# Second attention of a fused four-layer block: scores in pairs of heads

## The reference, cut to what matters

```python
# query: 8 x 112 x 512 (normalized x), key_value: 8 x 375 x 512 (context), 16 heads of 32
Q = query @ Wq.T + bq
K = key_value @ Wk.T + bk
V = key_value @ Wv.T + bv
# Q, K, V -> (batch, head, token, 32)
scores = jnp.einsum('bhsd,bhtd->bhst', Q, K) / np.sqrt(32)
attn = jax.nn.softmax(scores, axis=-1)
ctx = jnp.einsum('bhst,bhtd->bhsd', attn, V)
out = ctx.reshape(B, S, 512) @ Wo.T + bo
x = x + jnp.tanh(g_xattn[1]) * out
```

## Time and profile before

| | |
|---|---|
| median of three runs | 2813.0 us (2812.85 to 2819.16) |
| profiled execution, its own time | 2817.72 us |
| its span, first to last instruction | 2816.0 us |
| mean granted TensorE clock | 0.943 of full |
| busy: PE / DVE / ACT / POOL | 2568.2 / 932.3 / 656.2 / 450.9 us |

### The profile page before, as it was taken

The page is one execution under the profiler, slowest core; times in us unless marked ns, Lnnn a source line. Parts: engine busy times, 40 slices in busy tenths (PEclk is TensorE's granted clock), DMA queues, the critical chain, the costliest instruction groups (busy, mean ns, idle before and its releaser), DMA issues. The chain is left out here.

```text
span 2816.0 us, 35498 instructions
## 1 busy us (share of the span) xinstructions
PE 2568.2 (91%) x10573; PEld 1460.8 (52%) x10574; DVE 932.3 (33%) x2320; ACT 656.2 (23%) x1467; POOL 450.9 (16%) x607
## 2 busy tenths in 40 slices
PE   7999999999899888888898999959699999969988
PEld 4343434345455465665654556435356556434476
DVE  5232323234311333413451222464122222431275
ACT  2343424253011024324320111021011111042131
POOL 6000000000311200000023111414311111510062
PEclk9999999998999989899889999959799999979989
DMA  9101010002265310000042665423244453451220
GB/s 373 41 1 34 0 34 0 0 0 66 84 205 187 104 34 5 12 16 5 1 151 89 191 201 177 116 68 119 73 145 159 139 158 118 130 192 70 79 92 27
DMA packets 150025, 260.39 MB, mean 92 GB/s; under 512 B 16022, under 2 KB 80638, under 8 KB 149421
## 3 DMA queue, kind: packets, MB, share of 16 engines
q1 hardware_dynamic: 115885, 182.52, 19.9%
q0 software_dynamic: 19072, 49.35, 6.2%
q10 hardware_dynamic: 14976, 27.27, 2.5%
HBM read 209.21 MB, written 49.88 MB: 92 GB/s over the span
## 5 line engine op out<-in xcount | busy, mean ns | idle before, releaser
L360 POOL DMA_INDIRECT slot_list<-token_ids,slots x64 | 62.0, 969 | 725.7 <-DVEq L546 706.9
L1457 DVE CUSTOM_DVE_ANT_0 l0a_p<-bank,xn 112x375 f32<-112x375 f32 x128 | 70.3, 549 | 299.4 <-PE bank L1302 236.3
L250 PE MATMUL bank<-ident,xn 112*128 112x112 f32 x256 | 60.1, 403 | 86.2 <-DVE xn L226 86.2
L917 PE MATMUL bank<-f2r_wd,f2b_hT 128*128 (+1 forms) x300 | 137.2, 593 | 1.4 <-DVE f2b_hT L1006 1.4
L898 PE MATMUL bank<-f2r_wg,f2b_xT 128*128 x400 | 128.8, 466 | 1.5 <-ACT f2b_xT L954 1.3
L1330 PE MATMUL bank<-l0a_vo,l0a_zT 128*112 128x512 f32 x256 | 127.7, 593 | 0.0
L898 PE MATMUL bank<-f2r_wu,f2b_xT 128*128 x400 | 126.5, 459 | 0.0
L1404 ACT ACTIVATE l0a_p<-l0a_p,l0a_low 112x375 f32<-112x375 f32 x128 | 77.8, 608 | 191.8 <-DVE l0a_low L1466 191.8
L1302 PE MATMUL bank<-l_krT,l0a_qrT 64*112 64x375 f32 x256 | 112.8, 521 | 0.0
L360 POOL DMA_INDIRECT slot_list<-token_ids,slots_in x32 | 31.2, 974 | 499.4 <-DVEq L546 490.2
L1301 PE MATMUL bank<-l_kvcT,xnT 128*112 128x375 f32 x256 | 103.0, 484 | 2.8 <-ACT xnT L1399 2.8
(11 more groups left out here) (374 smaller groups left out, 4655.7 us busy)
## 6 DMA issues: line engine op xcount, KB each, us to landing
slot_rows<-zeros SPq DMA_DIRECT2D x2, 7424.0 KB
slot_rows<-f2b_y ACTq DMA_DIRECT2D x50, 256.0 KB, 3.7
f1r_wg<-in_l_wg SPq DMA_DIRECT2D x16, 704.0 KB, 4.6
f1r_wu<-in_l_wu SPq DMA_DIRECT2D x16, 704.0 KB, 6.6
f2r_wg<-in_l_wg SPq DMA_DIRECT2D x16, 704.0 KB, 4.4
f2r_wu<-in_l_wu SPq DMA_DIRECT2D x16, 704.0 KB, 6.0
xn<-in_l_w_ffn SPq DMA_DIRECT2D x11, 768.0 KB, 4.3
l_raw<-in_l_w_ffn SPq DMA_DIRECT2D x11, 768.0 KB, 4.4
```

Source lines behind the costliest of these rows:

```text
L250: mm = pe.transpose(s.bank[n % 4][:, k * TOK:(k + 1) * TOK], s.xn[:, n, k * 128:(k + 1) * 128], s.ident[0:TOK, 0:TOK])
L360: pool.indirect_dma_start(s.slot_list, bass.IndirectOffsetOnAxis(ap=slots[:, k, b:b + 1], axis=0), s.token_ids[:, b:b + 1], None, **bound) ...
L917: mm = pe.matmul(bank_y[v][:, :], hT[0:fn, v, c, :], wd[0:fn, bass.ds(at, 1), c, :].rearrange("p o f -> p (o f)"), start=(c == 0), stop=(c ...
L1457: dve.tensor_tensor_reduce(out=p[:, n % BUFS, :], in0=s.bank[n % 3][0:TOK, 0:T], in1=a.mask[:, b, :], scale=1.0, scalar=-3.0e38, op0=ALU.a ...
```

## The change

The scores of a batch are issued in two pairs of heads. Pair 0 (heads 0 and 1) stays at the head of the iteration and waits only for exponentials 0 and 1 of the batch before; pair 1 is issued after the mix of n-2 and before turnings 2 and 3, and waits for exponentials 2 and 3. DVE's iteration is put in another order: maximum of pair 0, divide n-2, maximum of pair 1, add n-4. ACT's list is unchanged.

```diff
-            def scores(g, b):
+            def scores(g, b, pair):
                 if b:
-                    pe.wait_ge(e_done, g * N + b * GH)
-                for j in range(GH):
+                    pe.wait_ge(e_done, g * N + (b - 1) * GH + 2 * pair + 2)
+                for j in (2 * pair, 2 * pair + 1):
...
                 for n in range(B + 3):
                     if n < B:
-                        scores(g, n)
+                        scores(g, n, 0)
                     if 0 <= n - 1 < B:
                         turn(g, n - 1, 0)
                         turn(g, n - 1, 1)
                     if 0 <= n - 2 < B:
                         mix(g, n - 2)
+                    if n < B:
+                        scores(g, n, 1)
                     if 0 <= n - 1 < B:
                         turn(g, n - 1, 2)
                         turn(g, n - 1, 3)
...
                 for n in range(B + 4):
+                    if n < B:
+                        maximum(g, n, 0)
+                    if 0 <= n - 2 < B:
+                        divide(g, n - 2)
+                    if n < B:
+                        maximum(g, n, 1)
                     if 0 <= n - 4 < B:
                         add(g, n - 4)
-                    if n < B:
-                        maximum(g, n, 0)
-                        maximum(g, n, 1)
-                    if 0 <= n - 2 < B:
-                        divide(g, n - 2)
```

## The result

The changed kernel takes 2880.5 us (median of four runs, 2875.9 to 2881.9) beside 2815.2 us for the kernel before on the same chip: ratio 1.0233, 95% interval 1.0216 to 1.025, slower by 65 us. The direction was forecast; the time lies above the range (2827 to 2875), and the forecast move of 35 us is little more than half of the measured one. The profiled execution has a span of 2878.8 us, 62.8 more than before.

The account below looks back on a forecast made before the run. The prediction took TensorE, busy 2568.2 of 2816.0 us, as the bound. Per group, -2.5 (start), +5.25 (batches 4 to 6), +2.5 (batch 7) and +3.4 (end) made +8.7 us, times four +35: 2848 us, range 2827 to 2875.

Parts of the forecast that it names:

- Step 1: Scores on PE in a steady period: splitting them takes away the 0.62 us of idleness before them.
- Step 2: Second scores block on PE: two heads cost 0.83 us, like four, so PE's own work sets some 5.5 us.
- Step 3: VectorE's queue: the add stands last, so the projection starts 3.18 us after pair 1 and waits 1.61 us.
- Step 4: Steady period of the inner loop: the chain through the late add takes 7.09 us, against 5.34 before.
- Head: Batches 0 to 3 of each group: 10.1 us at half clock, 21.8 us in all, a mean gain of 2.5 us.
- the bound "0": Lower bound of the gain in batches 0 to 3: none, if the second group's start keeps its 17.3 us of lower clock.
- Middle part: Steady periods, batches 4 to 6 of each group: 5.25 us longer, at a mean clock of 1.00.
- my first rival: The clock falls in the steady part too, mean 0.73: +23 us over 16 periods, 2871 us; chance 0.25.
- Tail: End of each group, after the last scores: adds lie 1.08 us behind divides, 3.4 us longer.
- Faster, if the add landed in time: Steady period: the projection finds bank 7 free, PE's 5.5 us set the period, 2805 us; chance 0.04.
- The clock does not fall in the head: Batches 0 to 3 of each group gain about 7.5 us instead of 2.5, giving 2828 us; chance 0.08.
- A pair costs half: Scores block of two heads on PE takes 0.42 us: about -2.8 us a group, 2837 us; no chance given.

Follow-up runs that it names:

- the add in front: The changed kernel with add n-4 put back first in VectorE's iteration; ratio 1.0009 to the kernel before.
- the filled version: The changed kernel with unused full-array products in the projection's wait and ahead of each group's second scores; ratio 1.0057 to the kernel before.
- changed kernel, add in front, head filled: The changed kernel with add n-4 first in VectorE's iteration and unused full-array products in each group's first gap; ratio 0.9926 to the kernel before.

## Why the prediction missed, point by point

*Step 1, the waits of the scores: right.* The 0.62 us are gone.

*Step 2, a pair costs as much as four: right.* The blocks take 0.82 us each (1082.14 to 1082.96), 0.83 before. The Trainium skill prices a pack as one matmul and some 4 ns for each further tile ("TensorE: Matmul & The Clock Gate", Measured speedup vs the span model), and the trace agrees. With the add in front PE's own work is seen alone: 5.45 us a period, 5.5 predicted.

*Step 3, the late add: right, in place and size.* The projection starts 3.16 us after pair 1 (1085.08 to 1088.24), 3.18 predicted. The cause is shown from both sides: with the add moved back the whole loss was gone, and the move alone made the kernel before slower by 1.2%.

*Step 4, the circle: right.* 7.11 us against 7.09.

*The sum: where it failed.* At full clock in all four loops, as the filled version shows, the changed schedule takes 55.5 us a loop; my steps give 16.7 + 3 x 7.09 + 7.09 + 10.6 = 55.7 to the last projection. (The four blocks of the head add up to 3.24 us, not to the 3.34 that I wrote: 0.3 us a group, 1 us in all, which changes nothing here.) So the schedule was sized right, and the clock was not, in three terms:

- *Head.* I took 10.1 us at the lower clock in each; measured are 13.7 to 17.1 (0.64 of full over 23.4 us). To the first scores of batch 4 the head takes 24.4, 22.3, 24.4 and 24.4 us instead of 21.8. The head's gain of 2.5 us a group, 10 in all, was nearly all lost: 8 to 9 us of it. I had the bound "0" for it, and took the mean of the gains at 10.1 us instead.
- *Middle part.* The likeliest case had it at full clock, 1.00. Two of four loops lost 2.9 and 8.0 us, 10.9 in all. This was my first rival; its +23 us were more than the middle part lost.
- *Tail.* I let only the wait grow, +3.4 us a group. From the fifth projection on it grew by 5.0, and each tail has 3.4 us at the lower clock; the same stretch at full clock is 11.5 us, 3.4 more than before. That is another 6.4 us, which neither the sum nor the rival had.

Together 26 us: 35 become 61. The term that failed is thus the clock: too little time at the lower level in the head, and none in the middle part and the tail. I had judged it from two rows, the stretch that held 1.00 with PE 73% busy and the one with a mean of 0.73 at 82% busy, and let the first decide. The two can't be compared in this way, because a block that takes PE 0.9 us at full clock takes it 1.6 at the lower level, which raises the busy share of the second. They left the question open, and that should have moved the middle of my forecast, not only its upper end. The two clock terms that I had priced, 10 us for the head's bound and 23 for the rival, would have given 2881 us together; that this is the measured time is in part luck, since the middle part lost 10.9 and not 23, and the tail had no such term.

The signs that I had named came out as follows: the period, the projection's wait, the scores without a wait and the price of a block as forecast; a head below 23 us only in one loop of four; and the lower clock in two middle parts, which was one of my signs of being wrong.

*Faster, if the add landed in time:* the version with the add in front tests that rival: not faster (1.0009) while the clock falls in the head, 0.7% faster where it doesn't. *The clock does not fall in the head:* it did, in all four loops. *A pair costs half:* no, by step 2.

## What to carry to other kernels

When an instruction moves in one engine's list, follow what it frees, not what it computes: a 0.75 us add that nobody waited for became the bound when it was put behind work that depends on the next stage of the same loop. Before a block is split, look whether its parts ran side by side; here they did, and each half cost what the whole had cost (0.82 and 0.83 us). And a new wait on TensorE is to be priced twice, once as time and once as clock; an idle stretch that can't be scheduled away can be filled with products that nobody reads. In the changed kernel that took 37 us off; in the kernel before it gained nothing, and the clock fell in the next gap instead.

## What was not expected of the hardware

- Waits of 1.44 us in a period of 7.11 us were enough to bring the clock down, but not each time: in 5 of 8 middle parts of the changed kernel, and in none of 8 when 1.3 us of the wait held full-array products. In the version with the add alone moved, waits of 1.20 us in a period of 6.08 brought it down in none of 4 middle parts. What decides was not isolated.
- The lower clock moved when the first gap was filled: in the kernel before, 10.2 us of it still stood in each head after most of the gap of 3.40 us had been taken by products.
- Once down, the clock stayed down through dense work: in the changed kernel's first head PE was busy 17.07 of 17.07 us at the lower level, after one gap of 2.33 us; in the other heads with this order on PE and the gap left open it was 13.7 to 20.5 us. The same scores, turnings and mixes ran at full clock when the gap had been filled (changed kernel, add in front, head filled), so this kind of work does not bring the clock down by itself. Whether it slows the return was not tested.

```profile
1053.50:1065.80 12.30, 12.30 (x156) 8.16 (x156) 7.87 (x15) 9.53 (x23) 0.00 (x0) 1.00 0.00 1
```
